# Two engines make the block products' weights in steps 11 to 22, and the block products begin with step 28 instead of 36

## What is computed

```python
# x: (32, 128, 512)  cond: (32, 512)  Wx, Wh: (512, 2048)  W_*, U_*, C_*: (512, 512)
xW = einsum('ntd,dg->ntg', x, Wx) + b
def lstm_step(h, c, xw_t):
    a = xw_t + h @ Wh                      # i, f, o, g: four gates of 512
    c = sigmoid(f) * c + sigmoid(i) * tanh(g)
    h = sigmoid(o) * tanh(c)
y = x + hs                                 # h starts as cond, c as 0
def gru_step(g, y_t):
    z = sigmoid(y_t @ W_z + g @ U_z + cond @ C_z + b_z)
    r = sigmoid(y_t @ W_r + g @ U_r + cond @ C_r + b_r)
    n = tanh(y_t @ W + (r * g) @ U + cond @ C + b)
    g = (1 - z) * g + z * n                # g starts as 0
out = y + gs
```

## Time and profile before

| | us |
|---|---|
| median of three runs | 1206.99 (1205.36 to 1207.92) |
| the profiled execution | 1206.86 |
| its span in the trace | 1205.1 |
| TensorE busy | 1176.5 (98%) |
| VectorE busy | 980.0 (81%) |
| ScalarE busy | 463.8 (38%) |
| GpSimd busy | 343.6 (29%) |

### The profile page before, as it was taken

The page is one execution under the profiler, slowest core; times in us unless marked ns, Lnnn a source line. Parts: engine busy times, 40 slices in busy tenths (PEclk is TensorE's granted clock), DMA queues, the critical chain, the costliest instruction groups (busy, mean ns, idle before and its releaser), DMA issues.

```text
span 1205.1 us, 75517 instructions
## 1 busy us (share of the span) xinstructions
PE 1176.5 (98%) x34486; PEld 859.5 (71%) x34486; DVE 980.0 (81%) x2904; ACT 463.8 (38%) x1117; POOL 343.6 (29%) x628
## 2 busy tenths in 40 slices
PE   5899999999999999999999999999999999999997
PEld 1467676666667777778777777777777777777775
DVE  2769778878878888888888888888888888888876
ACT  5565334344333333333333333333333333333332
POOL 3101233333222322322322233232232323323221
PEclk9899999999999999999999999999999999999999
DMA  9901311110011110111110011111001111101001
GB/s 313 327 10 21 143 21 22 21 21 9 17 21 21 22 22 6 20 22 21 22 22 16 10 21 22 21 22 22 11 15 22 22 21 22 21 9 18 13 13 21
DMA packets 142672, 44.17 MB, mean 37 GB/s; under 512 B 135888, under 2 KB 136144, under 8 KB 140816
## 3 DMA queue, kind: packets, MB, share of 16 engines
q1 hardware_dynamic: 140656, 38.68, 13.4%
q0 software_dynamic: 640, 0.53, 0.2%
q10 hardware_dynamic: 1056, 0.13, 0.1%
HBM read 30.93 MB, written 8.39 MB: 33 GB/s over the span
## 4 chain that ended last, share of the span: by engine, by line
PE 94%; SPq 3%; DMA 1%; DVE 1%; issue 0%; ACT 0%; DVEq 0%
PE ps_g L981 39%; PE ps_l L981 34%; PE ps_l L1044 15%; PE ps_g L990 3%; PE ps_c L1044 2%; SPq L298 2%; DMA o_area<-in_L_cond_C_dram 1%; PE ps_l L990 1%; SPq L302 1%; DVE zr L668 0%; SPq L309 0%; ACT zr L578 0%; DVE rg L901 0%; SPq L307 0%; DVE rgT L903 0%
## 5 line engine op out<-in xcount | busy, mean ns | idle before, releaser
L981 PE MATMUL ps_l<-wh,h2T 128*32 128x512 f16 x5952 | 344.4, 379 | 0.0
L981 PE MATMUL ps_g<-w,y2T 128*32 128x384 f16 x5760 | 256.1, 326 | 1.8 <-issue 1.8
L981 PEld LDWEIGHTS ps_l<-wh,h2T 128*32 128x32 f16 x5952 | 155.6, 97 | 133.5 <-issue 0.8
L981 PEld LDWEIGHTS ps_g<-w,y2T 128*32 128x32 f16 x5760 | 157.6, 97 | 91.3 <-issue 2.2
L423 POOL TENSOR_TENSOR yT<-xT,hT 128x128 f32<-128x128 f32 x128 | 61.8, 483 | 541.8 <-DVE hT L838 541.8
L981 PE MATMUL ps_g<-u,g2T 128*32 128x256 f16 x5760 | 179.1, 273 | 0.0
L981 PEld LDWEIGHTS ps_g<-u,g2T 128*32 128x32 f16 x5760 | 155.4, 97 | 15.3
L668 DVE SCALAR_TENSOR_TENSOR zr<-ps_g,sc,term 128x256 f32<-128x256 f32 x128 | 61.9, 483 | 80.0 <-PE ps_g L981 76.5
L376 POOL TENSOR_TENSOR o_area<-yT,gT 128x128 f32<-128x128 f32 x127 | 58.1, 458 | 192.3 <-DVE gT L962 191.4
L981 PE MATMUL ps_g<-u,rg2T 128*32 128x128 f16 x5760 | 102.4, 219 | 2.8 <-DVE rg2T L662 2.6
L606 ACT ACTIVATE g2T<-gT,sc 128x128 f16<-128x128 f32 x120 | 48.3, 402 | 131.7 <-DVE gT L962 131.7
(11 more groups left out here) (128 smaller groups left out, 1805.5 us busy)
## 6 DMA issues: line engine op xcount, KB each, us to landing
x_nat<-in_x_dram SPq DMA_DIRECT2D x126, 64.0 KB, 2.7
out_dram<-o_area SPq DMA_DIRECT2D x124, 64.0 KB, 2.0
wh<-in_L_cond_Wx_dram SPq DMA_DIRECT2D x4, 1024.0 KB, 10.9
stage<-in_L_cond_Wx_dram SPq DMA_DIRECT2D x4, 1024.0 KB, 9.2
w<-in_L_cond_Wh_dram SPq DMA_DIRECT2D x3, 1024.0 KB, 20.0
u<-in_L_cond_Wh_dram SPq DMA_DIRECT2D x1, 1024.0 KB, 24.8
stage<-in_L_cond_W_z_dram SPq DMA_DIRECT2D x1, 1024.0 KB, 8.7
stage<-in_L_cond_W_r_dram SPq DMA_DIRECT2D x1, 1024.0 KB, 8.0
```

The source lines that it names most:

```text
L981: mm = nc.tensor.matmul(bank[B * j:B * j + B, c0:c1].rearrange("p (n c) -> p n c", c=B), still(a, k), moving(b, k, j), start=opens and (a, ...
```

## The change

FW goes from 36 to 28, so that steps 28 to 35 too are computed with block products. The four differences are made by two engines: VectorE makes t1 and t2 (`make_t1`, `make_t2`), GpSimd t3 and t4 (`make_t3`, `make_t4`). With T_FIRST = 11 and T_SECOND = 15, a quarter of t1 is made in the ticks 11 to 14 and one of t3 in 12 to 15, one of t2 in 15 to 18 and one of t4 in 16 to 19. High halves on ScalarE: t1 in 11 to 14, t3 in 12 to 15, t2 in 16 to 19, t4 in 18 to 21. Low halves on VectorE: t1 in 11 to 14 and t2 in 16 to 19 behind `keep`, t3 in 13 to 16 and t4 in 19 to 22 behind the cell. The semaphores are one for each difference.

```diff
-    FW = 36
+    FW = 28
-        T_AGAIN, T_MADE = 9, 12
+        T_AGAIN, T_MADE = 9, 11
-        T_HIGH = {T_MADE + 1 + p + (p >= 2 * QUARTERS): p for p in range(4 * QUARTERS)}
-        T_LOW = {t + 1: p for t, p in T_HIGH.items()}
+        T_FIRST, T_SECOND = T_MADE, T_MADE + QUARTERS
...
+            def make_t3(p):
+                if p == 0:
+                    pool.wait_ge(again_in, 16 * K)
+                pool.wait_ge(t_made[T1], p + 1)
+                nc.gpsimd.tensor_tensor(quarter(t3, p), quarter(b22, p), quarter(b12, p), ALU.subtract).then_inc(t_made[T3], 1)
+            def make_t4(p):
+                pool.wait_ge(t_made[T2], p + 1)
+                nc.gpsimd.tensor_tensor(quarter(t4, p), quarter(b21, p), quarter(t2, p), ALU.subtract).then_inc(t_made[T4], 1)
...
-                if t in T_HIGH:
-                    t_high(T_HIGH[t])
+                if T_FIRST <= t < T_FIRST + QUARTERS:
+                    t1_high(t - T_FIRST)
+                if T_FIRST < t <= T_FIRST + QUARTERS:
+                    t3_high(t - T_FIRST - 1)
+                if T_SECOND < t <= T_SECOND + QUARTERS:
+                    t2_high(t - T_SECOND - 1)
+                if T_SECOND + 3 <= t < T_SECOND + 3 + QUARTERS:
+                    t4_high(t - T_SECOND - 3)
...
+            def make_t1(p):
+                if p == 0:
+                    dve.wait_ge(again_in, 16 * K)
+                nc.vector.tensor_tensor(quarter(t1, p), quarter(b12, p), quarter(b11, p), ALU.subtract).then_inc(t_made[T1], 1)
+            def make_t2(p):
+                dve.wait_ge(t_made[T1], p + 1)
+                dve.wait_ge(t_made[T3], p + 1)
+                nc.vector.tensor_tensor(quarter(t2, p), quarter(b22, p), quarter(t1, p), ALU.subtract).then_inc(t_made[T2], 1)
...
             def after_cell(t):
...
+                if T_FIRST + 1 < t <= T_FIRST + 1 + QUARTERS:
+                    t_low(N_T3, T3, t3, t - T_FIRST - 2)
+                if T_SECOND + 4 <= t < T_SECOND + 4 + QUARTERS:
+                    t_low(N_T4, T4, t4, t - T_SECOND - 4)
             def after_keep(t):
...
+                if T_FIRST <= t < T_FIRST + QUARTERS:
+                    t_low(N_T1, T1, t1, t - T_FIRST)
+                if T_SECOND < t <= T_SECOND + QUARTERS:
+                    t_low(N_T2, T2, t2, t - T_SECOND - 1)
             def tick(t, n, i):
...
+                if T_FIRST <= t < T_FIRST + QUARTERS:
+                    make_t1(t - T_FIRST)
+                if T_SECOND <= t < T_SECOND + QUARTERS:
+                    make_t2(t - T_SECOND)
...
                     if u == FW:
-                        pe.wait_ge(t_split, 4 * QUARTERS)
+                        for of in (T1, T2, T3, T4):
+                            pe.wait_ge(t_split[of], QUARTERS)
```

More of the change, by code:

```diff
@@ L156, in lstm_then_gru @@
         again_in = sem("again_in")
-        t_made = sem("t_made")
-        t_hi = sem("t_hi")
-        t_split = sem("t_split")
+        t_made = [sem(f"t{n + 1}_made") for n in range(4)]
+        t_hi = [sem(f"t{n + 1}_hi") for n in range(4)]
+        t_split = [sem(f"t{n + 1}_split") for n in range(4)]
         xs_done = sem("xs_done")
@@ L262, in lstm_then_gru @@
         N_T1, N_T3, N_T2, N_T4 = range(4)
+        T1, T2, T3, T4 = range(4)
         def parts(slab):
@@ L280, in in_pairs @@
             return xs[:, P * n:P * n + P].rearrange("p (m c) -> p m c", m=2)
-        T_AGAIN, T_MADE = 9, 12
+        T_AGAIN, T_MADE = 9, 11
         QUARTERS = 4
-        T_HIGH = {T_MADE + 1 + p + (p >= 2 * QUARTERS): p for p in range(4 * QUARTERS)}
-        T_LOW = {t + 1: p for t, p in T_HIGH.items()}
+        T_FIRST, T_SECOND = T_MADE, T_MADE + QUARTERS
         NG_W = FW // Q
-        assert max(T_LOW) <= FW - 5
+        assert T_SECOND + 2 * QUARTERS <= FW - 5
         def quarter(area, p):
-            return area[:, p % QUARTERS // 2, N2 // 2 * (p % 2):N2 // 2 * (p % 2 + 1)]
+            return area[:, p // 2, N2 // 2 * (p % 2):N2 // 2 * (p % 2 + 1)]
         @block.sync
@@ L394, in make_s @@
                 else:
-                    pool.wait_ge(t_split, 4 * QUARTERS)
+                    pool.wait_ge(t_split[T4], QUARTERS)
                 nc.gpsimd.tensor_tensor(s1, a21, a22, ALU.add).then_inc(xs_done, 1)
@@ L405, in tick @@
                 group = 2 * i + r
-                if T_MADE <= t < T_MADE + 4 * QUARTERS:
-                    if t == T_MADE:
-                        pool.wait_ge(again_in, 16 * K)
+                if T_FIRST < t <= T_FIRST + QUARTERS:
                     pool.wait_ge(g_lo, t - F)
-                    make_t(t - T_MADE)
+                    make_t3(t - T_FIRST - 1)
+                if T_SECOND < t <= T_SECOND + QUARTERS:
+                    pool.wait_ge(g_lo, t - F)
+                    make_t4(t - T_SECOND - 1)
                 if t > LAG:
@@ L497, in u_high, with t1_high, t3_high, t2_high @@
                 hi_part(u12[:, HI, :, g, :], by_gate(u_raw[g]), col["a_u"], u1_hi)
[L499 to L508, removed]
+            def t1_high(p):
+                act.wait_ge(t_made[T1], p + 1)
+                hi_part(quarter(t_parts[N_T1][:, HI], p), quarter(t1, p), col["a_wx"], t_hi[T1])
+            def t3_high(p):
+                act.wait_ge(t_made[T3], p + 1)
+                hi_part(quarter(t_parts[N_T3][:, HI], p), quarter(t3, p), col["a_wx"], t_hi[T3])
+            def t2_high(p):
+                act.wait_ge(t_split[T1], QUARTERS // 2)
+                act.wait_ge(t_split[T3], QUARTERS // 2)
+                act.wait_ge(t_made[T2], max(p + 1, QUARTERS // 2))
+                hi_part(quarter(t_parts[N_T2][:, HI], p), quarter(t2, p), col["a_wx"], t_hi[T2])
+            def t4_high(p):
+                act.wait_ge(t_split[T1], QUARTERS)
+                act.wait_ge(t_split[T3], QUARTERS)
+                act.wait_ge(t_made[T2], QUARTERS)
+                act.wait_ge(t_made[T4], p + 1)
+                hi_part(quarter(t_parts[N_T4][:, HI], p), quarter(t4, p), col["a_wx"], t_hi[T4])
             for k in range(K):
@@ L721, in u_low, with t_low @@
                 lo_part(u12[:, LO, k, g, :], by_gate(u_raw[g])[:, k], col["a_u"], u12[:, HI, k, g, :]).then_inc(u1_split, 1)
[L723 to L727, removed]
+            def make_t1(p):
[6 more added lines that the diff above has]
+                nc.vector.tensor_tensor(quarter(t2, p), quarter(b22, p), quarter(t1, p), ALU.subtract).then_inc(t_made[T2], 1)
+            def t_low(n, of, whole, p):
+                dve.wait_ge(t_hi[of], p + 1)
+                lo_part(quarter(t_parts[n][:, LO], p), quarter(whole, p), col["a_wx"], quarter(t_parts[n][:, HI], p)
+                        ).then_inc(t_split[of], 1)
             weight_scale(0, 0, K, "a_wx", wx_scale)
@@ L769, in after_cell @@
                     u_low(2, 0)
-                if t in T_LOW:
-                    t_low(T_LOW[t])
+                if T_FIRST + 1 < t <= T_FIRST + 1 + QUARTERS:
+                    t_low(N_T3, T3, t3, t - T_FIRST - 2)
+                if T_SECOND + 4 <= t < T_SECOND + 4 + QUARTERS:
+                    t_low(N_T4, T4, t4, t - T_SECOND - 4)
             def after_keep(t):
```

## The result

| | before | after |
|---|---|---|
| median of six runs, us | 1206.87 | 1215.24 (1213.76 to 1217.13) |
| the profiled execution, us | 1206.86 | 1215.74 |
| its span, us | 1205.1 | 1213.9 |

The changed kernel is slower: the ratio is 1.0065, 95% interval 1.0054 to 1.0076 (the two medians alone give 1.0069). The forecast was 1214.0 with a range of 1208.0 to 1217.5.

The account below looks back on a forecast made before the run. TensorE was taken to set the pace, with VectorE just keeping up. From the profiled 1206.86 us, 2.50 off for earlier block products and 9.64 added for TensorE's stalls gave 1214.0 us, range 1208.0 to 1217.5.

Parts of the forecast that it names:

- What bounds the kernel, and how much is in hand: TensorE sets the pace; if VectorE's zr starts over 0.41 us after TensorE had it ready, TensorE stands still.
- some 9.6 were named as the sign: Expected in the changed profile: TensorE's product on rg2T of step 22 starts about 9.6 us later than before.
- Part 1: Earlier block products: steps 28 to 35 turn from plain to block, 0.3125 us each, -2.50 us in all.
- The price of a make, 0.61: Each VectorE make in steps 11 to 18 delays ig_fc and the cell by 0.61 us, held up by GpSimd.
- The port pair: VectorE with two SBUF inputs and GpSimd reading SBUF take turns, so makes run one after the other.
- Part 3: ScalarE's high halves before the sigmoid of zr delay rg in steps 11 to 19; delays sum to 3.44 us.
- The sum: TensorE's stalls added over steps 11 to 22 from VectorE's need and ScalarE's delay: 9.64 us together.
- 36.61 - 3 x 9.11 = 9.28 once: TensorE's step is 9.11 us three times and 9.28 once per four, into steps 13, 17, 21, for scales.
- hidden makes: Rival, chance 0.19: GpSimd does not hold up VectorE's makes, six of eight fit into idle 0.59 us; 1210.5 us.
- faster: Rival, chance 0.06: VectorE's lateness is made up inside the step, only part 1 is left; 1204.4 us.
- More collisions: Rival, chance 0.16: late rg meets GpSimd's yT and late low halves y2T, 0.25 us in ten steps; 1216.5 us.
- The split: Rival, chance 0.01: the split is late and TensorE waits in step 25 a whole step of 9.1 us; 1223 us.

Follow-up runs that it names:

- the kernel with FW 36: The changed kernel with FW back at 36, so block products begin at step 36 as before; 1216.64 us against 1207.35 before, ratio 1.0079.
- without the weights' work: The changed kernel (FW 28) with no makes and no high or low halves, block products reading part of wx2; 1205.20 us, ratio 0.9978 to before.
- laid out by the rows: The changed kernel with late high halves and makes and low halves moved to steps with room, never two engines making in one; 1205.14 us, ratio 0.9981 to before.
- the late order: The changed kernel with ScalarE's high halves of t moved behind the high half of h; 1209.53 us, ratio 1.0015 to before.

## Why the prediction was right

- *What bounds the kernel, and how much is in hand.* Right. With a second low half and a make VectorE becomes the bound for ten steps, and in them TensorE waits for rg2T and nothing else. The 0.41 in hand reads 0.38 in the traces: where TensorE stood still, its product starts 1.02 behind rg (166.21, 167.23), and in step 14 before it was 1.39 (182.47, 183.86). The product of step 22 starts 9.68 later than before (266.77 against 257.09), where some 9.6 were named as the sign.
- *Part 1, -2.50.* Borne out in sign, and in size only to between 1.4 and 3.9. The traces point to the lower part of this: from the new h of step 24 to that of step 52 it is 253.42 before (273.35, 526.77) and 253.21 in the kernel with FW 36, against 251.97 in the changed kernel, 251.16 without the weights' work and 250.77 laid out by the rows, so 1.2 to 2.7 less. In the changed kernel itself it is 1.45 and not 2.50; single steps differ by 0.2 to 0.5 between executions, and no run tells how much of the difference is that.
- *The price of a make, 0.61.* Measured 0.60 in step 14, and 0.59 and 0.61 in steps 12 and 18. In steps 13, 15, 16 and 17 the cell comes only 0.45 to 0.52 later behind the gates' sums than before, since `ig_fc` took 0.63 to 0.69 there already, beside `add_out`: over the seven steps 0.55 less than forecast. The way to the price was slightly different too. I had GpSimd's `add_out` go ahead of the waiting make; in fact the make went first, `add_out` waited (0.91 in place of 0.46) and `ig_fc` waited for `add_out`. The three are done one after another either way, so the sum is the same. In steps 11 and 15 the makes read 0.65 and stand behind the turn of the output, as said; the one of step 15 moved the cell by 0.52.
- *The port pair.* By the Trainium skill (SBUF — State Buffer, section "SBUF: two separate sides") VectorE with two inputs in SBUF and GpSimd reading SBUF take one port pair in turn. The runs agree: a make takes 1.21 against 0.68, and the ratio for the whole kernel is 1.0027 against 1.0065 when GpSimd's makes go.
- *Part 3, ScalarE.* Right in mechanism, 1.99 from zr to rg in step 12 where 0.97 + 1.01 was forecast. The price was too small though. The forecast's own terms give 3.69 (3.44, and the 0.25 of step 11), and the late order was worth 5.7 us; steps 11 to 21 show 5.1 (110.20 from the product of step 10 to that of step 21, against 105.11). Most of it can be read on VectorE: over steps 11 to 19 the end of rg comes 4.4 later behind zr than with the late order. The delay by ScalarE is as forecast, 0.36 to 0.42 for two high halves beside a low half or one without, 1.03 in steps 12 and 18, and 0.16 in step 11, where 0.25 was taken; what the sum left out is that the late rg meets GpSimd's `yT` and takes 0.38 to 0.40 in steps 13, 14, 17 and 19 and 0.59 in step 11, where it takes 0.25 to 0.29 with the late order. The 0.6 from 5.1 up to 5.7 was not found in these steps.
- *The sum.* 9.64 forecast, 9.29 measured in the same terms; no step is off by more than 0.27. That it is so close is in part luck: the makes were priced 0.55 too high, and what the late rg loses beside GpSimd, 0.4 in these steps, was left out. The largest misses are step 12 (0.25 too little), step 21 (0.27 too much) and step 11, to which I gave 0: 9.30 from step 10, so 0.19, because GpSimd's `yT` met the rg that ScalarE had made late.
- *One term was booked in the wrong place.* "36.61 - 3 x 9.11 = 9.28 once" was laid to TensorE's small product for the scales. Without the weights' work the same steps take 9.10 to 9.14 with that product in them, so what is above this in the kernel before, 0.26 in step 13 (165.37, 174.74) and 0.14 in step 17, is not TensorE's own. It is a stall for VectorE, which comes to zr with nothing in hand there: in step 17 the product starts 1.02 behind rg, as it does where the changed kernel stalls. The two rows, of VectorE and of TensorE:

```profile
210.34 0.29 DVE L901 TENSOR_TENSOR rg<-zr,g_nat 128x128 f32<-128x128 f32 x1
```

```profile
211.36 0.85 PE L981 MATMUL ps_g<-u,rg2T 128*32 128x128 f16 x48
```

  It cancels in the forecast but for 0.1, since it stands in the time before as well (91.61 by the forecast's steps, 91.74 in the trace). But it means that the kernel before had no room in steps 13, 17 and 21, and that it loses 0.56 in these ten steps.
- *What doesn't add up.* The profiled execution after is 8.9 longer, and the ten steps (100.90 - 91.74 = 9.2), step 11 (0.2) and part 1 as forecast (-2.5) give 6.9. Of the 2.0 left, 0.34 is there by step 2 and 1.05 is part 1, which came to 1.45 in this trace. The last 0.65 comes behind step 52, where the same program runs: the new h of step 52 comes 8.25 later (535.02 against 526.77), that of step 127 8.90 later (1199.52 against 1190.62). Between 480 and 800 TensorE has two waits in the changed kernel, 0.4 for which the profile shows no cause and 0.3 for rg2T, and none before. The granted clock reads 1.00 in both from 147 on, so it isn't that. Single steps that are 0.2 to 0.5 longer occur in both kernels, in other places each time. What makes them isn't shown. The medians differ by 8.4. So the forecast is 1.2 under the median with its main term right and a part 1 that was, in this trace, about 1 too large.

Of the rivals, hidden makes and faster are refuted by the makes' 1.21 and by the result. More collisions are there but are small, 0.7 in all with step 11. The split wasn't late: no wait on it is in TensorE's list, and step 25 lasts 9.43, against 9.44 without the weights' work.

## What to carry to other kernels

Before work is handed to a second engine that runs "at the same time", look whether both read two operands from the same memory: VectorE and GpSimd did theirs one after the other, and the waiting fell on the critical one. Count for every step what the engine next to the bound needs for itself, in the order in which it does it, and how much of a step is left; an engine with 19% idle had 0.4 us of room in one step and none in another. Work that nobody waits for goes behind the instruction that somebody waits for, and into the places where the timeline shows a wait: with the same work laid out so, the same goal gave 0.19% instead of costing 0.65%.

## What was unexpected of the hardware

- Here the instruction that had waited went first. When GpSimd's make ended at 183.96, its next instruction `add_out` (shown from 183.91) and VectorE's make both stood ready; VectorE's was done at 184.51 and `add_out`, which had waited since, at 184.82, ahead of VectorE's next, `ig_fc`. In all six steps in which the two makes meet it is so (`add_out` 0.90 to 0.92, VectorE's make 1.21).
- Four makes in a row on VectorE take 2.49, 0.62 each, with 0.68 to 0.69 shown for each: an instruction starts before the one in front of it has ended by the trace, which is the reason to count from start to start.
